# Moving the gating of a finished chunk one scan step forward, and the squaring of its projection one step back

## The reference, cut to what matters

```
u, z = split(x @ in_proj.T)                       # 256 channels each, u goes through a convolution and silu
dt, B, C = ...                                    # from u; 16 states
for each token:
    s = s * exp(dt * A) + (dt * u) * B            # 256 channels x 16 states
    y = sum over the 16 states of s * C
y = (y + u * D_skip) * silu(z)                    # the gate
out = y @ out_proj.T                              # then: residual, rms norm, a three-layer MLP
```

## Time and profile before

| | us |
|---|---|
| median of 3 runs | 1578.76 (1577.99 to 1582.11) |
| profiled execution, its own time | 1578.67 |
| its span from first to last instruction | 1576.8 |
| busy: TensorE, VectorE, ScalarE, GpSimd | 1336.3, 1202.2, 1027.1, 914.7 |

### The profile page before, as it was taken

One profiled execution on the slowest core, in us unless ns is written; L12 is line 12 of the kernel. 1 busy time (PEld: TensorE's weight loads), 2 busy tenths in 40 slices (PEclk: granted clock), 3 DMA queues, 4 the chain that ended last, 5 costly groups with the idle time before them and its releaser, 6 DMA issues.

```text
span 1576.8 us, 23586 instructions
## 1 busy us (share of the span) xinstructions
PE 1336.3 (85%) x8074; PEld 727.1 (46%) x8090; DVE 1202.2 (76%) x1740; ACT 1027.1 (65%) x1732; POOL 914.7 (58%) x476
## 2 busy tenths in 40 slices
PE   6786596578578888888888889999999999999987
PEld 2344486233123333333333455555555555555553
DVE  2895353486799999999997688888888888888862
ACT  4464254687545555555553688888888888888863
POOL 0356244000799899899983566665556566656540
PEclk9875699897789999999999999999999999999999
DMA  3301221200443434336531212011212111211100
GB/s 118 92 12 33 58 67 51 77 1 12 98 113 91 103 100 103 93 99 181 157 109 36 48 28 48 20 43 28 48 28 48 28 43 33 48 41 34 36 21 27
DMA packets 71069, 96.76 MB, mean 61 GB/s; under 512 B 13683, under 2 KB 32422, under 8 KB 70694
## 3 DMA queue, kind: packets, MB, share of 16 engines
q1 hardware_dynamic: 68646, 90.51, 22.3%
q0 software_dynamic: 2304, 4.74, 0.9%
HBM read 63.73 MB, written 8.41 MB: 46 GB/s over the span
## 4 chain that ended last, share of the span: by engine, by line
PE 47%; DVE 12%; ACT 11%; issue 7%; POOL 2%; DMA 0%; SPq 0%; DVEq 0%; ACTq 0%; POOLq 0%
PE at_two L1883 7%; DVE ssm_state L1562 6%; PE glu_bank L1819 5%; PE at_one L1979 4%; PE ssm_bank L1250 4%; DVE ssm_seen L1571 4%; ACT home_dt L2088 4%; PE glu_bank L1800 4%; PE at_two L1861 3%; PE at_two L1913 3%; PE at_one L1891 3%; PE glu_bank L1845 2%; PE ssm_bank L1284 2%; POOL ssm_dbu L1465 1%; PE ssm_bank L1247 1%
## 5 line engine op out<-in xcount | busy, mean ns | idle before, releaser
L1465 POOL TENSOR_TENSOR ssm_dbu<-ssm_dtu,ssm_b_all 128x1024 f32<-128x1024 f32 x128 | 297.7, 2359 | 29.8 <-DVE home_dt L1526 29.4
L2098 POOL TENSOR_TENSOR at_direct<-at_direct,home_u 128x1024 f32<-128x1024 f32 x64 | 151.0, 2359 | 274.9 <-DVE home_u L2189 274.9
L1391 ACT ACTIVATE ssm_bank<-home_dt,ssm_decay 128x512 f32<-128x512 f32 x256 | 174.6, 690 | 152.5 <-DVE ssm_state L1562 151.0
L1250 PE MATMUL ssm_bank<-ssm_seen,ident 128*128 128x512 f32 x512 | 247.3, 607 | 27.8 <-DVE ssm_seen L1571 23.4
L1250 PEld LDWEIGHTS ssm_bank<-ssm_seen,ident 128*128 128x128 f32 x512 | 96.4, 194 | 146.1 <-issue 85.4
L1562 DVE TENSOR_TENSOR_SCAN ssm_state<-ssm_bank,ssm_carry,ssm_dbu 128x512 f32<-128x512 f32 x128 | 155.7, 1265 | 9.4 <-ACT ssm_bank L1391 9.4
L1562 DVE TENSOR_TENSOR_SCAN ssm_state<-ssm_bank,ssm_dbu 128x512 f32<-128x512 f32 x128 | 147.9, 1206 | 15.3 <-ACT ssm_bank L1391 7.8
L2103 POOL TENSOR_TENSOR home_z<-home_z,at_inv 128x1024 f32<-128x1024 f32 x64 | 121.4, 1897 | 18.7 <-DVE at_inv L2200 18.7
L1883 PE MATMUL at_two<-home_u,at_hs 128*128 128x512 f32 x256 | 125.7, 614 | 7.7 <-ACT at_kT L2026 5.5
L2226 DVE TENSOR_REDUCE at_peak<-at_scores 128x8 f32<-128x1024 f32 x64 | 78.2, 1222 | 62.3 <-PE at_scores L1946 51.0
L2109 POOL TENSOR_TENSOR at_direct<-at_direct,at_rnorm 128x1024 f32<-128x1024 f32 x64 | 121.8, 1903 | 0.2
(11 more groups left out here) (248 smaller groups left out, 3094.6 us busy)
## 6 DMA issues: line engine op xcount, KB each, us to landing
ssm_b_all<-ssm_b_rows SPq DMA_DIRECT2D x128, 256.0 KB, 3.4
at_v_mix<-at_v SPq DMA_DIRECT2D x112, 128.0 KB, 2.3
ssm_c_all<-ssm_b_rows SPq DMA_DIRECT2D x40, 256.0 KB, 3.7
at_hs<-branch SPq DMA_DIRECT2D x64, 128.0 KB, 2.3
moe_w<-in_moe_w SPq DMA_DIRECT2D x16, 256.0 KB, 6.0
gru_scan<-moe_to_experts SPq DMA_DIRECT2D x40, 64.5 KB, 1.8
x<-in_x SPq DMA_DIRECT2D x8, 256.0 KB, 3.7
branch<-moe_from_experts SPq DMA_DIRECT2D x8, 256.0 KB, 5.1
```

What stands on the lines that cost most here:

```text
L1250: last = nc.tensor.matmul(bank[Y0 + half][:], ident[:], seen[:, n % 2, half], start=False, stop=n == STATES - 1)
L1391: nc.scalar.activation(bank[DA0 + half][:], chunk_of(dt[:, half], t), ACT.Exp, scale=decay[:, half, n:n + 1]).then_inc(r[f"da{half}"], 1)
L1465: nc.gpsimd.tensor_tensor(dbu[:, i % RING], dtu[:, t % 2], b_all[:, i % B_RING:i % B_RING + 1, :].broadcast_to([P, 2, CH]), ALU.mult).then ...
L2098: nc.gpsimd.tensor_tensor(direct[:, n % TURNED], direct[:, n % TURNED], crossed[n % 2], ALU.add).then_inc(s["added"], 1)
```

## The change

Two numbers change. The gate goes from `at` = -2 to -3, so that it stands in front of scan(1) of the next chunk. The squaring and the copy go from `at` = 1 to 2, so that they stand behind the decays of state 4. Nothing is added or taken away, and TensorE, GpSimd and SyncE have the same lists as before.

```
-                t = posted(i, 1)
+                t = posted(i, 2)
                 if t is not None:
                     act.wait_ge(r["out"], up_to(t))
                     nc.scalar.activation(chunk_of(dt[:, 0], t), bank[W0][:], ACT.Square
...
             for i in range(LAST_STEP + 1):
-                t = posted(i, -2)
+                t = posted(i, -3)
                 if t is not None:
                     dve.wait_ge(r["y"], up_to(t * STATES + STATES - 1))
                     for half in range(2):
```

## The result

The changed kernel takes 1595.66 us (median of 4 runs, 1592.18 to 1598.0) against 1578.38 us before (1577.56 to 1582.11): ratio 1.0103, 95% interval 1.0078 to 1.0128. Measured again with the experiments, the same pair gave 1.0073 (1.0050 to 1.0097). By the medians it is slower by 12 to 17 us; the forecast was 12.4, so that the first measurement lies 4.6 us above the 1591.1 foretold. Executions of the changed kernel differ: of the six in the second measurement four took 1589.5 to 1590.2 us, and two, the profiled one among them, 1596.9 and 1598.1. Both traces of the changed kernel are of long executions (1598.0 and 1596.9 us), so what is read from them explains the long ones; what is different in a short one no trace shows.

The account below looks back on a forecast made before the run. VectorE was taken as the bound, with GpSimd close behind. Order at full clock (+2.6 us) plus TensorE's low clock (+9.8 us) gave +12.4 us on 1578.7, so 1591.1 us, 0.8% slower; range 1580 to 1597.

Parts of the forecast that it names:

- What bounds: In a scan chunk VectorE is the bound, GpSimd close behind; a change is worth its effect on VectorE's idle time.
- The squaring: Decays of state 4 no longer stand behind it; all 17.2 us of VectorE's wait can go if nothing else is late.
- The wait in front of the gate: VectorE idles in front of the earlier gate until y(15) is done, 1.7 to 1.9 us at seven boundaries.
- y(0) late, GpSimd behind it: Late y(0) delays seen(2), and GpSimd's chain delays scan(8): +0.54 us odd, +1.13 even boundaries; +2.6 us in all at full clock.
- a sign of being wrong: A scan(8) that does not wait for GpSimd, or a clock of 1.0 in the scan, would make the prediction wrong.
- The clock: TensorE's joined 4.0 us gap brings the low clock at all seven boundaries, 1.4 us each, +9.8 us.
- the 1.7 and 1.8 of the rows: Price of one low-clock fall read from the profile: 1.7 us at the fourth boundary, 1.8 from four products taking 3.78.
- my upper bound of 2.5: Most that one fall costs, in us, where the slow stretch covers most of the chain and the projection too.
- the time that half of the low stretch gives: By the skill's rule alone, price is half the low-clock time behind each gap; the prediction equated this with its forecast time.
- The costly rival: Clock stays low through the projection; y(1), seen(3) and decays of state 5 wait too: 2.5 us a boundary, 1599 us, chance 0.12.
- its 20 us: Total slowdown if the slow stretch costs more: 2.6 us plus 17.5 us over the boundaries.
- The sum: 2.6 + 9.8 = 12.4 us slower, all of it through GpSimd to scan(8).

Follow-up runs that it names:

- e1_square_only: Kernel before with only the squaring a step later, the gate left in front of scan(2); ratio 0.9953 to the kernel before, 7.5 us faster.
- two filling products: Changed kernel with two idle matmuls in TensorE's gap in front of `pick` of state 1 at each boundary; ratio 1.0061 to the kernel before.
- e3_fill: Changed kernel with three idle matmuls filling TensorE's gap in front of `pick` of state 1 at each boundary; ratio 1.0030 to the kernel before, 1583.1 us.

## Why the prediction was right

- *What bounds.* Right. VectorE's work did not change, and its idle time decided.
- *The squaring.* Right: the 17.2 us of waits for decays are gone. `e1_square_only` shows that they are worth 7 us and not 17 when GpSimd's chain follows; 8 had been worked out, and the even boundaries did not give their part.
- *The wait in front of the gate.* Foretold 1.7 to 1.9 us, measured 1.64 to 2.10.
- *y(0) late, GpSimd behind it.* Foretold +1.13 at even, +0.54 at odd boundaries; the periods at full clock give +1.12 (55.38 against 54.26) and +0.44 (55.94 against 55.50). The seventh was mis-sized: its period with the filling is 55.28 against 55.28, 0.0 instead of +0.54. The last chunk has no next one, so the dt * u of 2.31 us is missing from GpSimd's chain, and scan(8) does not wait for GpSimd there, which the prediction had named as a sign of being wrong. With it the sum is +1.8 and not +2.6. Like the recorded one, it is counted against a kernel before whose clock fell twice; with the clock full on both sides the order costs 5.2 us.
- *The clock.* The mechanism was right: the low clock behind the joined gap delays seen(2), and GpSimd's chain hands the delay on. The step "so I take 1.4. Seven times that is **+9.8 us**" was mis-sized. It took something off the 1.7 and 1.8 of the rows because part of a slow stretch may lie in the gap. Six boundaries fell and not seven. Two falls lasted 3.4 us, with nothing of them in the gap; four lasted 6.8, of which 1.1 to 1.7 us lay in the gap and the rest, 5.1 to 5.7, behind it. Measured against the periods at full clock, the six cost 2.79, 2.52, 2.55, 1.70, 1.71 and 2.58, 13.9 in all. The four long ones lie above my upper bound of 2.5, by up to 0.3. The working also calls the forecast the time that half of the low stretch gives; half of 3.4 us is 1.7 and not 1.4, which would have made 1593.2.
- *The costly rival.* Its price of 2.5 was right for four boundaries; its 20 us did not come, since two falls were short and one boundary held. Its reason was not: seen(3) waited as well at all six (the 14.1 us of waits for line 1235, less 0.5 in the first chunk), but at the first six boundaries scan(8) starts 16.24 to 16.29 us behind seen(2) with and without that wait, so the wait is the same delay and not one more. At the seventh alone it is what carries the delay.
- *The sum.* 1.8 + 13.9 = 15.6 us in the scan (by rounding), against 12.4 foretold. With the clock full on both sides as the measure, 5.2 of it are the order and 10.4 the clock (13.9 less the 3.4 that two falls cost before). The sum lies between the forecast and the costly rival. That the second measurement gave 12 us is no better hit of the working: it comes from executions that no trace shows, and the number of falls differs from one execution to the next (two and one in the traces of the kernel before). So the direction and the path were foreseen, and how near the number came is in part luck.

The Trainium skill, "TensorE: Matmul & The Clock Gate", section "Why this matters for your kernels", says that long idle gaps between bursts bring the half rate; the traces agree behind gaps of 3.9 to 4.9 us (19 of the 21 in three profiles fell), and they show falls behind shorter ones, too.

## What to carry to other kernels

Moving an instruction earlier in one engine's list to release another engine's work helps only if that work can start; here the next thing in TensorE's list waited for something that the move made later. Look at what stands between the released work and its engine's present place, and move that as well. When a change joins two short gaps of TensorE into one, count the low clock behind it as a cost, and when an engine's wait is moved, follow the first late result through the list of the engine with the least slack.

## What the runs showed that I had not expected

The fall of the clock depends on more than the length of one gap. Behind a gap of 4 us it held twice in 14 boundaries, the fourth one in both profiles of the changed kernel; with two filling products (2.2 to 2.3 us left, 3.15 at the first boundary) it fell at 5 of 7, and with three (1.3 to 1.4 us, 2.29 at the first) at none. In the kernel before, with 0.8 to 1.5 and 0.9 us in two pieces, it fell at 2 of 7 in one execution and at 1 of 7, another one, in the next. Where it falls it stays low for 3.4 or 6.8 us. And a fall can come elsewhere: in `e1_square_only` and `e3_fill` the clock held at most boundaries, and then fell in the middle of five chunks behind 2.4 us of idle, at 1.4 to 1.6 us each. What decides between a gap behind which the clock falls and one behind which it holds stays open.
